# Graph mixture-of-experts kernel, edge stage: ScalarE's single rows fetched one round ahead, VectorE's and ScalarE's order inside a group changed

## The chip, the core and the metric

The kernel runs on one core of a Trainium2 chip. The metric is the device time of one execution in microseconds (us). Three executions of the kernel before took 2914.96, 2916.74 and 2917.04 us; the median is 2916.74 us.

## The reference, cut to what matters

`x` holds 6250 nodes of 256 features, `src` and `dst` 200000 edges sorted by `dst`. All arithmetic is float32.

```python
h = feats * rsqrt(deg_out)[:, None]
m = segment_sum(h[src], dst, num_segments=n) * rsqrt(deg_in)[:, None]
x1 = (m @ W_gc + b_gc) + (feats @ W_res + b_res)
# top-2 of 64 experts, each gelu(x @ w1 + b1) @ w2 + b2
y = x1 + moe(x1)
# normalise over nodes, add feats, LayerNorm over features
```

The change touches only the stage that computes `segment_sum(h[src], dst)`, the projection of each finished tile of 128 nodes and its routing to experts.

## The kernel before, in words

**Ahead of the edge stage** the kernel counts out-degrees, scales the nodes and writes them to `table` in HBM. SyncE (SP) issues those stores. For each group of edges it packs the first and last tile of nodes that the group's edges reach, and how many tiles are finished after it, into one integer, `code` (line 904).

**The edge stage** takes the edges in 196 groups of 1024 (`GROUPS`), each of 8 chunks of 128 (`CPG`). A round (`it`) is six groups, `q` = 0 to 5 (`RING`), and there are six ring buffers. Five engines work on it, each with its own loop:

- GpSimd (POOL) gathers one chunk of 128 rows of 1 KB per indirect DMA (line 516). It waits for the indices of the group (`idx_ready`) and for the sum of the group six before (`acc_added`, line 513), since that frees the buffer. In the sixth group (`q` = 5, `ROW_Q`) it gathers seven chunks; the rows of the eighth are fetched one by one by two other engines, so a round has 47 gathers.
- SP fetches 96 of these 128 rows with one DMA each into `row_buf` (lines 413 to 423) and then counts `rows_there`. It does so for round `it` once `rows_placed` says that round `it` - 2 was placed.
- ScalarE (ACT) per group: makes the indices for the same buffer of the next round (line 638), runs the group's tick if it has one, and in `q` = 0 to 3 loads 8 node numbers and issues 8 row DMAs straight into the ring buffer of `q` = 5 (lines 693 to 695). It can't start them before the last round's sixth group is summed (line 690). At the end of `q` = 3 it copies SP's 96 rows from `row_buf` into the ring buffer (line 702, `rows_placed`).
- VectorE (DVE) makes for each group the one-hot matrices that send an edge's row to its node: `dstq` (line 923) and `hot` (line 925), two buffers. If the group reaches a second tile it makes a second set, `dstx` and `hotx` (lines 934 and 936). It adds TensorE's results to `acc` (line 943 for the second tile, line 1048 for the first, which counts `acc_added`).
- TensorE (PE) multiplies the 8 one-hot matrices with the 8 gathered chunks (line 1258), called the main product below, and once more with `hotx` for a second tile. For `q` = 5 it also waits for `rows_placed` and `act_rows` (lines 1331 and 1332).

**A tick** follows a group that finishes a tile `i` (each group with a second tile here). All engines but POOL take part: ACT copies `x` and the tile's sums to `xS` and `mS` (lines 642 and 644) once `acc_added` has this group; DVE takes the in-degree (line 962) for ACT's square root (line 646). PE transposes four blocks (line 1275), and does the rank products of tile `i` - 2 (lines 1282 and 1283). ACT copies them to `tS` (line 650) and PE projects (line 1296). For tile `i` - 1 DVE forms `yS` (lines 971 and 973), PE transposes it (line 1289), ACT copies it to `ytS` (line 654), and PE computes the logits (line 1303). DVE does the placing of tile `i` - 2 (lines 980 to 1005), the choice of experts of tile `i` - 1 (from line 1012), and ends with a reciprocal (line 1029), after which ACT refines the root (lines 665 to 671).

**The order on VectorE** before, in `extras` and `pair`: load the group's code (line 309) and branch on it (line 944); if there is a second tile, make `hotx`, then (`later`) the one-hots of the next group, then wait for the second product and add it; without a second tile, only the one-hots of the next group. Then wait for the main product, add it (line 1048), and run the tick.

**After the edge stage** POOL waits for all 196 sums (line 526), clears its buffers (lines 527 to 529) and waits for the slot tables (line 532); then the experts run.

Of the kernel before, what the change touches and what calls it, by code (L numbers as in the profile page):

```python
# [9 lines left out]
ALU = mybir.AluOpType  # L10
# [4 lines left out]
P = 128  # L15
# [26 lines left out]
ACT_TURNS = (P - SP_ROWS) // ACT_ROWS  # L42
MAIN = 3
# [19 lines left out]
def graph_moe_kernel(nc, x, src, dst, W_gc, b_gc, W_res, b_res, Wg, bg, w1, b1, w2, b2, gamma, beta, out):  # L63
    ctx = ExitStack()
    with ctx:
# [531 lines left out]
        def _(act):  # L597
# [42 lines left out]
            def tick(i, behind, sums=GROUPS):  # L640
# [14 lines left out]
                behind(1, transposed_y)  # L655
                def keep_y(t):
# [16 lines left out]
            def group_ticks(g):  # L673
                ticks_of_group(act, group_code(act, g), lambda i, behind: tick(i, behind, g + 1))

# [7 lines left out]
            def fetch_rows(it, par, turn, first):  # L683
                r0 = SP_ROWS + turn * ACT_ROWS
                if turn == 0:
                    if first:
                        act.wait_ge(table_first, 16)
                        act.wait_ge(table_rest, 16 * (NB - 1))
                    else:
                        act.wait_ge(acc_added, it * RING)  # L690
                    act.wait_ge(listed, it * 16 + 16)
                    act.sem_inc(act_starts, 1)
                act.load(row_regs, row_list[0:1, bass.ds(par, 1), r0:r0 + ACT_ROWS])
                for r in range(ACT_ROWS):
                    act.dma_start(ring(ROW_Q)[r0 + r:r0 + r + 1, CPG - 1, 0:D], row_of(act, row_regs[r])).then_inc(act_rows, 16)  # L695
# [9 lines left out]
            def step(it, first):  # L705
                par = 0 if first else nc.s_assert_within(act.snap(it & 1), 0, 1,
                                                         skip_runtime_bounds_check_because="it is a parity")
# [770 lines left out]
```

## Time and profile before

| | |
|---|---|
| median of three runs | 2916.74 us |
| the profiled execution's own time | 2912.62 us |
| its span in the profile | 2910.8 us |
| busy share of the span | PE 71%, PEld (weight loads) 59%, DVE 42%, ACT 15%, POOL 64% |
| granted TensorE clock, mean | 0.833 of full |
| edge stage (first gather to last sum) | 210.05 to 2161.7 us |

The profile is one execution; times count from the start of its span. A row of the timeline gives the start, the duration, engine and line, the operation, and in brackets how long the engine had been idle and what ended that.
### The profile page before, as it was taken

Reading aid. Unit: us, or ns where it says so; the run is one execution under the profiler, and the core shown is the slowest. Engines: PE = TensorE matmul, PEld = TensorE weight load, DVE = VectorE, ACT = ScalarE, POOL = GpSimd, SP = SyncE. Lnnn points to the kernel's source line nnn. Section 1 sums busy time; section 2 is a strip of 40 time slices with the busy share of each in tenths; the row PEclk is TensorE's granted clock in tenths of the full one; section 3 lists DMA queues with packets and bytes.
Section 4 is the critical chain, followed back from the end, with each engine's and each line's share of the span. In section 5 each row is a group of like instructions: output and inputs, shape, how many; then the busy total and the mean of one; then the engine's idle time right before and its main releaser. Section 6 shows DMA issues by size and latency. Waiting matters only on the chain.

```text
span 2910.8 us, 57770 instructions
## 1 busy us (share of the span) xinstructions
PE 2063.8 (71%) x10204; PEld 1716.3 (59%) x10251; DVE 1223.3 (42%) x3115; ACT 444.0 (15%) x1390; POOL 1855.4 (64%) x1938
## 2 busy tenths in 40 slices
PE   8955556556666666767777768777766799999760
PEld 7954444445455555555556556565646788899650
DVE  8971112222323434344445455454553322222367
ACT  3010000000000101111111111111112223333213
POOL 0007777777777777777777777777715767777500
PEclk6557777888888878888988899998888999999885
DMA  8033333333333333333333333333314556666532
GB/s 301 0 99 109 109 108 107 108 110 109 109 109 110 112 109 110 111 111 111 113 111 113 112 113 113 112 115 112 112 31 139 168 166 204 198 197 202 188 113 88
DMA packets 211682, 361.84 MB, mean 124 GB/s; under 512 B 46696, under 2 KB 133558, under 8 KB 211534
## 3 DMA queue, kind: packets, MB, share of 16 engines
q0 software_dynamic: 92112, 226.49, 26.4%
q1 hardware_dynamic: 110266, 126.48, 13.5%
q10 hardware_dynamic: 9156, 7.48, 0.8%
q14 instruction: 127, 1.04, 0.1%
q8 instruction: 21, 0.34, 0.0%
HBM read 327.93 MB, written 57.52 MB: 132 GB/s over the span
## 4 chain that ended last, share of the span: by engine, by line
POOL 38%; PE 23%; issue 19%; DVE 9%; DMA 5%; DVEq 4%; ACTq 1%; POOLq 1%; ACT 1%; PEld 1%; SPq 0%; PEldq 0%
POOL ring L516 19%; POOL stage L516 18%; PE bank L1258 6%; PE bank L1379 6%; PE bank L1373 6%; PE bank L1238 3%; DMA y<-ring,slots 1%; DMA ring<-nodes,slots 1%; DMA stage<-y 1%; PE bank L1364 1%; DVE acc L1156 1%; DVE stage L839 1%; POOL y L551 1%; PEld bank L1448 1%; ACTq L695 1%
## 5 line engine op out<-in xcount | busy, mean ns | idle before, releaser
L516 POOL DMA_INDIRECT ring<-table,ring_idx x792 | 749.0, 946 | 242.1 <-issue 240.9
L516 POOL DMA_INDIRECT stage<-table,ring_idx x739 | 698.9, 946 | 225.1 <-issue 224.0
L1258 PE MATMUL bank<-stage 128*128 128x257 f32 x1030 | 323.1, 482 | 195.9 <-DMA stage<-table,ring_idx 87.1
L1258 PE MATMUL bank<-ring,hot 128*128 128x257 f32 x1056 | 316.1, 465 | 164.9 <-DMA ring<-table,ring_idx 119.2
L1258 PEld LDWEIGHTS bank<-stage 128*128 128x128 f32 x1030 | 249.9, 249 | 263.7 <-issue 132.4
L1258 PEld LDWEIGHTS bank<-ring,hot 128*128 128x128 f32 x1056 | 245.3, 238 | 229.5 <-issue 111.6
L1048 DVE TENSOR_TENSOR acc<-acc,bank 128x257 f32 x196 | 82.9, 423 | 491.1 <-PE bank L1258 464.2
L1373 PEld LDWEIGHTS bank<-ring,stage 128*128 128x128 f32 x1984 | 237.8, 197 | 9.7 <-issue 3.1
L1373 PE MATMUL bank<-ring,stage 128*128 128x128 f32 x1984 | 240.4, 281 | 2.4 <-DVE ring L1103 1.1
L1258 PE MATMUL bank<-ring,stage 128*128 128x257 f32 x528 | 170.6, 493 | 95.8 <-DMA ring<-table,ring_idx 70.7
L551 POOL DMA_INDIRECT y<-ring,slots x192 | 194.9, 1015 | 65.5 <-issue 48.6
L1379 PE MATMUL bank<-stage,ring 128*128 128x256 f32 x976 | 225.1, 384 | 8.8 <-ACT ring L737 7.3
L1258 PE MATMUL bank<-stage,hot 128*128 128x257 f32 x512 | 158.2, 476 | 91.5 <-DMA stage<-table,ring_idx 71.7
L1258 PEld LDWEIGHTS bank<-ring,stage 128*128 128x128 f32 x528 | 131.6, 256 | 132.3 <-issue 71.1
L1379 PEld LDWEIGHTS bank<-stage,ring 128*128 128x128 f32 x976 | 182.1, 192 | 34.1 <-issue 10.9
L1258 PEld LDWEIGHTS bank<-stage,hot 128*128 128x128 f32 x512 | 122.4, 245 | 124.9 <-issue 58.7
L737 ACT ACTIVATE ring<-bank,b1e 128x128 f32<-128x128 f32 x488 | 139.1, 368 | 356.3 <-PE bank L1373 356.3
L638 ACT ACTIVATE ring_idx<-srcT 128x8 int32 (+1 forms) x198 | 40.4, 206 | 930.2 <-DMA ring<-table,ring_idx 448.6
L541 POOL DMA_INDIRECT ring<-nodes,slots x129 | 137.3, 1064 | 67.7 <-issue 41.0
L1238 PE MATMUL bank<-stage 128*128 128x49 bf16 x1568 | 160.6, 279 | 6.6 <-DVE stage L839 5.7
L1238 PEld LDWEIGHTS bank<-stage 128*128 128x128 bf16 x1568 | 153.2, 150 | 14.1 <-DVE stage L839 13.6
L923 DVE TENSOR_SCALAR dstq<-dstT,neg_base 128x8 f32 (+1 forms) x196 | 48.7, 249 | 246.1 <-issue 240.8
(231 smaller groups left out, 2479.6 us busy)
## 6 DMA issues: line engine op xcount, KB each, us to landing
stage<-in_L_gnn_w_dram SPq DMA_DIRECT2D x128, 512.0 KB, 4.0
row_buf<-table SPq DMA_DIRECT2D x3072, 1.0 KB
stage<-table ACTq DMA_DIRECT2D x1024, 1.0 KB
ring<-table,ring_idx POOLq DMA_INDIRECT x792
y<-zeros SPq DMA_DIRECT2D x49, 256.0 KB, 2.4
stage<-y SPq DMA_DIRECT2D x14, 896.0 KB, 7.1
stage<-table,ring_idx POOLq DMA_INDIRECT x739
stage<-in_L_gnn_b_dram SPq DMA_DIRECT2D x64, 128.0 KB
```

The source lines that it names most:

```text
L516: pool.indirect_dma_start(out=ring(q)[:, j, 0:D], out_offset=None, in_=table[:, :], in_offset=bass.IndirectOffsetOnAxis(ap=ring_idx[:, q, ...
L541: pool.indirect_dma_start(out=xg[e % AHEAD][:, k, :], out_offset=None, in_=nodes[:, :], in_offset=bass.IndirectOffsetOnAxis(ap=gidx[:, col ...
L551: pool.indirect_dma_start(out=y2[:, :], out_offset=bass.IndirectOffsetOnAxis(ap=sidx[:, col:col + 1], axis=0), in_=outs[:, par, k, :], in_ ...
L638: act.activation(ring_idx[:, q, :], srcT[:, bass.ds((it * RING + q) * CPG, CPG)], ACT.Copy).then_inc(idx_ready, 1)
L695: act.dma_start(ring(ROW_Q)[r0 + r:r0 + r + 1, CPG - 1, 0:D], row_of(act, row_regs[r])).then_inc(act_rows, 16)
L737: last = act.activation(h1[:, k, j, :], banks[2 + k][:, j * P:(j + 1) * P], ACT.Gelu, bias=b1e[:, j:j + 1])
L923: dve.tensor_scalar(dstq[:, q, :], dstT[:, bass.ds(g * CPG, CPG)], neg_base[:, bass.ds(g, 1)], None, ALU.add)
L1048: dve.tensor_tensor(acc[:, bass.ds(first_tile, 1), :], acc[:, bass.ds(first_tile, 1), :], banks[q][:, 0:D + 1], ALU.add).then_inc(acc_adde ...
L1238: last = pe.matmul(banks[0][:, 0:HI], lo_hot[:, q, :, c], hi_hot[:, q, :, c], start=first and q == 0 and c == 0, stop=final and q == n - 1 ...
L1258: last = pe.matmul(bank[:, 0:D + 1], hots[:, j, :], ring(q)[:, j, :], start=j == 0, stop=j == n - 1)
L1373: last = pe.matmul(bank[:, j * P:(j + 1) * P], w1s[:, par, c, j * P:(j + 1) * P], xt[:, c, :], start=c == 0, stop=c == DK - 1)
L1379: last = pe.matmul(dst, h[:, j, :], w2s[:, par, j, :], start=j == 0, stop=j == HK - 1)
```

## The change

- ACT fetches its 32 single rows for round `it` + 1 in `q` = 1 to 4 of round `it`, into `row_buf` (now all 128 partitions), not into the ring. Those of round 0 are fetched ahead of all groups.
- ACT places all 128 rows with one copy at `q` = 1 (`PLACE_Q`) of the round, in round 0 at `q` = 4. That copy now waits for the sum of the last round's sixth group and for its own rows; PE no longer waits for `act_rows`.
- VectorE makes the one-hots of the next group first, before it loads the group's code. The second tile's rows come after that in a loop over the further tiles, with one more drain.
- In a tick ACT copies `mS` after DVE's in-degree (`nd_deg`), not after `acc_added`; and it copies `ytS` before `tS`, where it was the other way round.

```diff
@@ scalar: tick @@
                 if i is not None:
                     act.activation(xS[:, :], xs[:, bass.ds(i, 1), :], ACT.Copy)
-                    act.wait_ge(acc_added, sums)
+                    act.wait_ge(nd_deg, i + 1)
                     act.activation(mS[:, :], acc[:, bass.ds(i, 1), 0:D], ACT.Copy).then_inc(nd_in, 1)
-                    act.wait_ge(nd_deg, i + 1)
                     act.activation(tmp[:, bass.ds(i, 1)], deg[:, bass.ds(i, 1)], ACT.Sqrt).then_inc(nd_sqrt, 1)
-                if i is not None:
-                    act.wait_ge(nd_tr, i + 1)
-                    act.activation(tS[:, :, :], banks[3][:, :], ACT.Copy).then_inc(nd_t, 1)
                 def transposed_y(t):
                     act.wait_ge(nd_ytr, t + 1)
                     act.activation(ytS[:, :, :], banks[5][:, 0:D], ACT.Copy).then_inc(nd_yt, 1)
                 behind(1, transposed_y)
+                if i is not None:
+                    act.wait_ge(nd_tr, i + 1)
+                    act.activation(tS[:, :, :], banks[3][:, :], ACT.Copy).then_inc(nd_t, 1)
@@ scalar: rows @@
-            def fetch_rows(it, par, turn, first):
+            def fetch_rows(it, par, turn):
                 if turn == 0:
-                    if first:
-                        act.wait_ge(table_first, 16)
-                        act.wait_ge(table_rest, 16 * (NB - 1))
-                    else:
-                        act.wait_ge(acc_added, it * RING)
                     act.wait_ge(listed, it * 16 + 16)
...
-                    act.dma_start(ring(ROW_Q)[r0 + r:r0 + r + 1, CPG - 1, 0:D], row_of(act, row_regs[r])).then_inc(act_rows, 16)
+                    act.dma_start(row_buf[r0 + r:r0 + r + 1, bass.ds(par, 1), :], row_of(act, row_regs[r])).then_inc(act_rows, 16)
...
-            def place_rows(it, par):
+            def place_rows(it, par, first):
+                if not first:
+                    act.wait_ge(acc_added, it * RING)
+                    act.wait_ge(act_rows, it * (16 * (P - SP_ROWS)) + 16 * (P - SP_ROWS))
                 act.wait_ge(rows_there, it + 1)
-                act.activation(ring(ROW_Q)[0:SP_ROWS, CPG - 1, 0:D], row_buf[0:SP_ROWS, bass.ds(par, 1), :],
-                               ACT.Copy).then_inc(rows_placed, 1)
+                act.activation(ring(ROW_Q)[:, CPG - 1, 0:D], row_buf[:, bass.ds(par, 1), :], ACT.Copy).then_inc(rows_placed, 1)
...
-                    group_ticks(it * RING + q)
-                    if q < ACT_TURNS:
-                        fetch_rows(it, par, q, first)
-                    if q == ACT_TURNS - 1:
-                        place_rows(it, par)
+                    ticks_of_group(act, group_code(act, it * RING + q), tick)
+                    if q == (ROW_Q - 1 if first else PLACE_Q):
+                        place_rows(it, par, first)
+                    if rows and q > PLACE_Q - 1 and q - PLACE_Q < ACT_TURNS:
+                        fetch_rows(it + 1, other, q - PLACE_Q)
@@ vector @@
-            def extras(g, c, later):
+            def extras(g, c):
                 first_tile, last_tile = field(dve, c, 0), field(dve, c, 1)
-                    rows_of(second)
-                    later()
-                    sum_of(second)
...
+                with dve.If(last_tile > first_tile):
+                    with dve.Fori(first_tile + 1, last_tile + 1) as tile:
+                        t = a_tile(tile)
+                        dve.reg_add(extra, extra, 1)
+                        n = dve.snap(extra, min_val=1, max_val=GROUPS * NT)
+                        dve.drain()
+                        dve.tensor_scalar(dstx[:, :], dstT[:, bass.ds(g * CPG, CPG)], neg_tile[:, bass.ds(t, 1)], None, ALU.add)
+                        dve.drain()
+                        dve.tensor_tensor(hotx[:, :, :], ...).then_inc(hotx_ready, 1)
+                        dve.drain()
+                        dve.wait_ge(groupx_mm, n)
+                        dve.tensor_tensor(acc[:, bass.ds(t, 1), :], acc[:, bass.ds(t, 1), :], banks[2][:, 0:D + 1], ALU.add)
@@ vector: pair @@
-                    def later(q=q):
-                        if q + 1 < HOTS:
-                            one_hots(it, q + 1)
-                        elif not final:
-                            one_hots(it + 1, 0)
+                    if q + 1 < HOTS:
+                        one_hots(it, q + 1)
+                    elif not final:
+                        one_hots(it + 1, 0)
                     c = group_code(dve, g)
-                    first_tile = extras(g, c, later)
+                    first_tile = extras(g, c)
@@ tensor @@
                     if q == ROW_Q and not final:
                         pe.wait_ge(rows_placed, it + 1)
-                        pe.wait_ge(act_rows, it * (16 * (P - SP_ROWS)) + 16 * (P - SP_ROWS))
```

## Rows read from the trace of the kernel before

**Rows 1.** Waits of POOL: engine, line, waited for: us in total, times, longest.
```profile
POOL ring L516 <- issue: 240.9, 788, 1.0
...
POOL ring L527 <- DVE acc L1048: 38.0, 1, 38.0
```

**Rows 2.** Stretches, gathers of line 516: stretch, length, busy (count), PEclk, DMA share, GB/s.
```profile
208.00:1980.00 1772.00, 1338.64 (x1416) 0.84 0.38 110
208.00:2124.40 1916.40, 1447.92 (x1531) 0.84 0.38 110
```

**Rows 3.** The same stretches, sums of line 1048.
```profile
208.00:1980.00 1772.00, 75.69 (x179) 0.84 0.38 110
208.00:2124.40 1916.40, 80.76 (x191) 0.84 0.38 110
```

**Rows 4.** Timeline: sums of groups 179, 187, 189, 193; 193's tick ends.
```profile
1989.65 0.42 DVE L1048 TENSOR_TENSOR acc<-acc,bank 128x257 f32 x1 [0.26 <-issue]
...
2080.61 0.42 DVE L1048 TENSOR_TENSOR acc<-acc,bank 128x257 f32 x1 [0.26 <-issue]
...
2101.92 0.42 DVE L1048 TENSOR_TENSOR acc<-acc,bank 128x257 f32 x1 [0.26 <-issue]
...
2148.75 0.42 DVE L1048 TENSOR_TENSOR acc<-acc,bank 128x257 f32 x1 [0.26 <-issue]
...
2156.60 0.16 DVE L1029 RECIPROCAL rs<-tmp  x1
```

**Rows 5.** Timeline, groups 188 and 189: VectorE and TensorE.
```profile
2088.74 0.16 DVE L1029 RECIPROCAL rs<-tmp  x1
...
2090.60 0.23 DVE L923 TENSOR_SCALAR dstq<-dstT,neg_base 128x8 f32 x1 [1.70 <-issue]
...
2090.91 1.23 DVE L925 TENSOR_TENSOR stage<-bank,dstq 128x1024 f32<-128x1024 f32 x1
2092.19 5.42 PE L1258 MATMUL bank<-stage 128*128 128x257 f32 x16 [3.30 <-DVE stage L925]
2092.42 0.42 DVE L1048 TENSOR_TENSOR acc<-acc,bank 128x257 f32 x1 [0.29 <-issue]
...
2094.26 0.23 DVE L934 TENSOR_SCALAR dstx<-dstT,neg_tile 128x8 f32 x1 [1.41 <-issue]
...
2097.45 3.64 PE L1258 MATMUL bank<-stage,slots 128*128 128x257 f32 x16
```

**Rows 6.** Chain of waits: VectorE's sequencer (DVEq) between that reciprocal and the one-hots.
```profile
2089.25 0.32 DVEq L309
...
2090.33 0.04 DVEq L922
```

**Rows 7.** Stretches: PE, PEld, DVE, ACT, POOL busy (count), PEclk, DMA share, GB/s.
```profile
1950.60:1954.40 3.80, 3.75 (x16) 2.95 (x16) 1.66 (x3) 0.21 (x1) 2.84 (x3) 1.00 0.36 107
...
2092.20:2096.00 3.80, 3.80 (x10) 3.04 (x11) 2.02 (x4) 0.21 (x1) 2.89 (x4) 0.56 0.36 105
```

**Rows 8.** Waits of TensorE for the single rows (the row is named by its destination).
```profile
PE bank L1258 <- DMA stage<-table: 60.3, 11, 7.0
```

**Rows 9.** Timeline, group 191: TensorE.
```profile
2116.80 5.27 PE L1258 MATMUL bank<-stage 128*128 128x257 f32 x16 [6.51 <-DMA stage<-table]
```

**Rows 10.** Timeline, the tick around the sum at 2101.92: VectorE and ScalarE.
```profile
2100.84 0.42 ACT L642 ACTIVATE xS<-xs 128x256 f32 x1 [1.02 <-issue]
...
2102.58 0.15 DVE L962 TENSOR_SCALAR deg<-acc  x1 [0.24 <-issue]
...
2103.72 0.60 ACT L650 ACTIVATE tS<-bank 128x512 f32<-128x512 f32 x1 [0.65 <-PE bank L1275]
...
2104.55 0.38 ACT L654 ACTIVATE ytS<-bank 128x256 f32<-128x256 f32 x1 [0.24 <-PE bank L1289]
...
2107.84 0.22 DVE L1012 TENSOR_TENSOR lg<-bank,bgb 128x64 f32<-128x64 f32 x1
```

**Rows 11.** Timeline, SyncE: the single-row DMAs of one round.
```profile
1982.15 44.77 SPq L420 DMA_DIRECT2D row_buf<-table  x96
```

More of the change, by code:

```diff
@@ L638, in indices, with tick @@
                 act.activation(ring_idx[:, q, :], srcT[:, bass.ds((it * RING + q) * CPG, CPG)], ACT.Copy).then_inc(idx_ready, 1)
[L640 removed]
+            def tick(i, behind):
                 if i is not None:
                     act.activation(xS[:, :], xs[:, bass.ds(i, 1), :], ACT.Copy)
[L643 removed]
+                    act.wait_ge(nd_deg, i + 1)
                     act.activation(mS[:, :], acc[:, bass.ds(i, 1), 0:D], ACT.Copy).then_inc(nd_in, 1)
[L645 removed]
                     act.activation(tmp[:, bass.ds(i, 1)], deg[:, bass.ds(i, 1)], ACT.Sqrt).then_inc(nd_sqrt, 1)
[L648 to L650 removed]
                 def transposed_y(t):
@@ L710, in step @@
                     indices(it + ahead // RING, ahead % RING, first and ahead < RING)
-                    group_ticks(it * RING + q)
-                    if q < ACT_TURNS:
-                        fetch_rows(it, par, q, first)
-                    if q == ACT_TURNS - 1:
-                        place_rows(it, par)
+                    ticks_of_group(act, group_code(act, it * RING + q), tick)
[3 more added lines that the diff above has]
+                        fetch_rows(it + 1, other, q - PLACE_Q)
+            act.wait_ge(table_first, 16)
+            act.wait_ge(table_rest, 16 * (NB - 1))
+            for turn in range(ACT_TURNS):
+                fetch_rows(0, 0, turn)
+            act.wait_ge(act_rows, 16 * (P - SP_ROWS))
             step(0, True)
-            with act.Fori(1, STEPS - 1) as it:
+            with act.Fori(1, STEPS - 2) as it:
                 step(it, False)
+            step(STEPS - 2, False, False)
             it = STEPS - 1
             for q in range(LASTQ):
-                group_ticks(it * RING + q)
+                ticks_of_group(act, group_code(act, it * RING + q), tick)
             last_ticks(act, tick)
@@ L926, in one_hots @@
                                   dstq[:, q, :].unsqueeze(2).to_broadcast([P, CPG, P]), ALU.is_equal).then_inc(hot_ready, 1)
-            def extras(g, c, later):
+            def extras(g, c):
                 first_tile, last_tile = field(dve, c, 0), field(dve, c, 1)
-                def rows_of(t):
-                    dve.drain()
-                    dve.tensor_scalar(dstx[:, :], dstT[:, bass.ds(g * CPG, CPG)], neg_tile[:, bass.ds(t, 1)], None, ALU.add)
-                    dve.drain()
-                    dve.tensor_tensor(hotx[:, :, :], iota_ps.unsqueeze(1).to_broadcast([P, CPG, P]),
-                                      dstx[:, :].unsqueeze(2).to_broadcast([P, CPG, P]), ALU.is_equal).then_inc(hotx_ready, 1)
-                def sum_of(t):
-                    dve.reg_add(extra, extra, 1)
-                    n = dve.snap(extra, min_val=1, max_val=GROUPS * NT)
-                    dve.wait_ge(groupx_mm, n)
-                    dve.tensor_tensor(acc[:, bass.ds(t, 1), :], acc[:, bass.ds(t, 1), :], banks[2][:, 0:D + 1], ALU.add)
-                with dve.If(last_tile > first_tile):
-                    second = a_tile(first_tile + 1)
-                    rows_of(second)
-                    later()
-                    sum_of(second)
-                    with dve.If(last_tile > first_tile + 1):
-                        with dve.Fori(first_tile + 2, last_tile + 1) as tile:
-                            t = a_tile(tile)
-                            rows_of(t)
-                            sum_of(t)
-                with dve.Else():
-                    later()
@@ new lines, in extras @@
+                with dve.If(last_tile > first_tile):
+                    with dve.Fori(first_tile + 1, last_tile + 1) as tile:
[5 more added lines that the diff above has]
+                        dve.drain()
+                        dve.tensor_tensor(hotx[:, :, :], iota_ps.unsqueeze(1).to_broadcast([P, CPG, P]),
+                                          dstx[:, :].unsqueeze(2).to_broadcast([P, CPG, P]), ALU.is_equal).then_inc(hotx_ready, 1)
+                        dve.drain()
+                        dve.wait_ge(groupx_mm, n)
+                        dve.tensor_tensor(acc[:, bass.ds(t, 1), :], acc[:, bass.ds(t, 1), :],
+                                          banks[2][:, 0:D + 1], ALU.add)
```

10 lines of the change are left out of this document (5 added, 5 removed).

## The prediction

> **What bounds the kernel now.** I read the waits of POOL first. The 1531 gathers [rows 2] take 1448 us and stand 0.305 us apart for no reason but issue [rows 1]: one gather each 1.25 us. Nothing in the change touches them, so POOL sets the pace of the stage up to 2124.4 us, and most work saved on other engines there is worth nothing. But then POOL waits 38.0 us for the last sum [rows 1]. Counting gathers against sums shows why. At 1980 us 1416 gathers are issued and 179 groups summed, which used 29 x 47 + 5 x 8 = 1403 of them; at 2124.4 it is 1531 against 191 groups, 1497 gathers [rows 2, 3]. So the backlog grows from 13 to 34 gathers (43 us). The other engines are slower than POOL in the last stage, where a tile ends with nearly every second group, and what they owe is paid after the last gather. **The lag of a group** is the time from its last gather's end to its sum. Gathers after group 193 take (8 + 3) x 1.25 = 13.8 us, so its gathers ended at 2110.6; its sum stands at 2148.75 [rows 4]: lag 38.2. For group 179 (121 gathers before the end: 1973.1; sum 1989.65) it is 16.6. Only this lag can be won.
>
> **What one cycle is made of.** From 179 to 193 there are seven pairs of a plain group and one with a second tile and a tick. They take 159.1 us; their gathers 137.6 (19.7 a pair). Pair 188/189, from the sum at 2080.61 [rows 4]: VectorE's tick ends with the reciprocal 8.1 later, the one-hots start after 1.86 more and are ready at +11.5, TensorE starts the main product at +11.6, the second product 5.26 after that, and the sum follows 4.5 after its start [rows 5]: 21.3. TensorE was idle for 3.30 us ahead of the main product, and the granted clock over it is 0.56, mostly the 1.2 GHz level; the same product of an earlier pair (group 176) ran at 1.00, the 2.4 GHz level, in 3.75 us [rows 7], where its follower can start after some 3.5. So the order alone costs 21.3 - (5.26 - 3.5) = 19.5, hardly more than the gathers, and the fallen clock 1.8. A third cost comes once a round: ScalarE's last eight single rows arrive late where the tick falls on q = 3. Group 191 starts at 2116.80 [rows 9], while its one-hots were due 11.6 after 2101.92, at 2113.5: 3.3 us lost. TensorE's waits for these rows are 60.3 us in 11 rounds [rows 8], with idling in it that it would have had anyway; the late ones among the last groups are 179, 185 and 191. Per pair that adds up: 159.1 / 7 = 22.7 is 19.5 + 1.8 + 0.9 (two waits of 3.3 in seven pairs), and 0.5 where the clock fell for longer.
>
> **The change, part by part.**
> *Rows a round ahead.* ScalarE's eight loads and DMAs per turn stay 32 per round; the three late arrivals (3 x 3.3 = 9.9) go. New in their place: the copy at q = 1 waits for the sum of the last group of the round before, and behind it stand ScalarE's fetches, the indices and the next tick. Indices are a round ahead of POOL, so this costs nothing while the lag is under five groups; if that cover were gone, POOL would stop. Copying 128 rather than 96 partitions I take at 0, as the copies of both heights in this trace have 0.42 us a piece; bounds 0 to 0.1. SP's 96 DMAs take 44.8 us [rows 11] of a round of 47 x 1.25 = 58.8, and are released two groups earlier than now; I count it as nothing. In round 0 the fetch for round 1 at q = 1 waits for the list that SP loads after its first 96 rows, some 27 us; group 5 may start 2 to 3 us late, at a lag of 8 that closes again: 0.
> *One-hots first.* After a tick they no longer wait for code, fields and branch: 2090.33 - 2089.25 = 1.08 us [rows 6]. Main product at +10.5 rather than +11.6.
> *Second tile's rows later.* The plain group's sum comes at +10.7; the next one-hots 0.8 after it (1.84 [rows 5] less the moved 1.03) and take 0.3 + 1.23. In their shadow run code, branch and the loop's set-up; `dstx` starts 1.3 (nothing but the drain) to 2.3 (all register work behind it) after them, I take 1.6, as the register steps of [rows 6] fit beside 1.23 us of work. Then 0.3 + 1.23: `hotx` ready at +15.0. The main product ends at +14.0 at full clock, at +15.7 as in [rows 5]. So the second product starts at +15.0 or +15.7, the sum comes at 19.5 or 20.2.
> *Tick order.* `mS` waits for the in-degree at 2102.58 + 0.15: 0.4 later. TensorE's transposes and rank products move by as much, and VectorE, which uses these at once, by 0.3. `ytS` then ends near 2105.0 [rows 10], `tS`, now behind it, takes 0.60, and the projection starts at 2105.7, 1.3 later than now; the logits end at +6.1, where VectorE wants them at 2107.84 - 2101.92 = +5.92 [rows 10] plus that 0.3. So 0.3 a tick; bounds 0 and 1.3 (all of TensorE's delay). TensorE's next plain product, 1.3 later, ends at +9.7 and waits only about 1.1 us for the one-hots, not 3.3. That is where I expect the clock to stay up: the waits of 1.0 us inside ticks leave it at 1.00 now.
> *ScalarE between ticks at q = 1 and 3* has two fetches, as before. Its `xS` ends at 2101.26 [rows 10], 0.66 ahead of the sum. With a pair 0.8 to 1.5 shorter, a tick that ends 0.3 later and an `mS` due 0.4 later, it is late by 0 to 0.8; I take 0.3.
>
> **The sum.** With the tick's 0.3 a pair comes to 19.8 (clock up) or 20.5; with ScalarE's lateness in two pairs of three I take 20.7, the worse end, since I can't exclude falls elsewhere. Seven pairs: 144.9 - 137.6 = 7.3 us of growth instead of 21.5. At group 179 the lag is 16.6 less 3.3 for the rows, less 1.3 for the clock (1.8, damped since such a wait doesn't always cost it): 12.0 (the floor is about 10: 2.1 landing, 3.5 and 4.5 for the products). So 19.3 at group 193 instead of 38.2: 18.9 less. The last tick gives back 0.3, and one tick more runs beside gathers: 0.3 by their lengths (2088.74 - 2080.61 = 8.13 beside, 2156.60 - 2148.75 = 7.85 after the last, [rows 4, 5]). By the Trainium skill, "SBUF — State Buffer", section on who interferes with whom, VectorE and GpSimd share a port pair and the second to come "fully blocks"; with 0.95 us a gather, the tick's eight bf16 scalar operations could then lose up to 7.6 us in that one tick more, and the gain would be near 11. The two tick lengths don't bear that out. Total: -18.9 + 0.3 + 0.3 = -18.3. Against the profiled execution's own 2912.6 that gives 2894.3; the median of before is 4.1 above that execution, so against it 2898.4.
>
> **Rivals.**
> *Only the row waits go* (0.14). The clock falls as often as now, because the waits of TensorE only move into the tick and ahead of `hotx`, and the order gives nothing. For it: the second product waits 1.0 us more. Against: 1.08 us saved sit on the chain itself. Gain 9.9: 2906.8.
> *ScalarE becomes the bound* (0.07). It now has four fetches between q = 1 and 4, each 5.5 with the group's code; if tick and fetches leave it 2.0 late at each tick, it gives back 7 x 2.0 = 14 and the result is within noise: 2912 to 2918. For it: the estimate above is already 0.3 late. Against: between two ticks it has no more fetches than now, and it is 15% busy over the span.
> *Slower: the tick's new order* (0.06). Place: between `ytS` and the logits. If the clock falls in the longer gap ahead of the projection, projection and logits (2.4 us) double, VectorE waits for the logits 2.4 + 0.3 per tick and saves 1.08: 1.6 lost per pair, 7 pairs after 179 and some 5 before it that now don't recover, 12 x 1.6 = 19 less 9.9 for the rows: +9, 2926. It decides from the point where a tick grows by more than 1.08 + 9.9/12 = 1.9 us. Against it: waits of 1 us keep the clock up now.
> *The change doesn't do what it says* (0.03): TensorE waits for ScalarE at the round's last group as before, now for the copy; 2916.
>
> **Numbers.** Forecast 0.70 and its rivals 0.30. A measurement of this kernel can tell 0.2%, 5.8 us, from no change. Low end: 19.8 a pair, the clock always up, is a growth of 1.0 and a lag of 13.0, less 25.2 and 0.6 back: 2892. High end takes in the second rival's time and some of ScalarE's: 2911. Faster 0.85, same 0.09, slower 0.06.
>
> **What would show it.** Right: POOL's wait for line 1048 falls from 38 to about 19 us; no wait of TensorE for single rows; 188/189 takes 20 to 21 us, with a wait of about 1 us ahead of the main product and PEclk near 1.0 over it; reciprocal to `dstq` 0.8 instead of 1.86; `hotx` about 3 us after the hot's start; tick 8.4 long. The gathers keep 1.25 us. Wrong: ticks of 9 us or more, ScalarE's `mS` over 1.5 us after the sum, or a backlog at 2124 us still above 30 gathers.

## The result and the profile after

| | before | after |
|---|---|---|
| median of four runs | 2916.9 us | 2959.0 us |
| ratio, 95% interval | | 1.014 (1.0121 to 1.0159) |
| profiled execution's own time, span | 2912.6, 2910.8 | 2954.9, 2953.1 |
| gathers done | 2124.4 | 2153.7 |
| last sum | 2161.7 | 2200.8 |

The change makes the kernel 42 us slower, where 18 us less was forecast. I read the changed kernel's profile as the one before: first what POOL waits for.

Waits of the kernel after: engine, line, waited for: us in total, times, longest.

```profile
ACT ring_idx L639 <- issue: 836.0, 144, 32.2
PE bank L1263 <- ACT mS L645: 160.3, 49, 11.3
DVE junk L970 <- PE bank L1271: 98.6, 17, 10.5
DVE lg L1002 <- PE bank L1291: 55.5, 27, 6.3
POOL ring L528 <- DVE acc L1036: 47.8, 1, 47.8
POOL stage L517 <- ACT ring_idx L639: 19.7, 9, 7.8
POOL ring L517 <- ACT ring_idx L639: 9.8, 9, 6.1
```

The same view of the kernel before has these for them.

```profile
ACT ring_idx L638 <- issue: 283.0, 80, 5.3
PE bank L1275 <- ACT mS L644: 52.7, 49, 2.0
DVE lg L1012 <- PE bank L1303: 4.0, 3, 2.8
```

The wait for the last sum has grown by 47.8 - 38.0 [rows 1] = 9.8 us, and POOL now waits 19.7 + 9.8 = 29.5 us for ScalarE's gather indices, where it waited 0.3. Together 39.3; the last sum stands 39.1 later. The other rows name the engine behind both. TensorE waits three times as long for ScalarE's `mS`. VectorE stands 98.6 us for the rank products behind that transpose, where it stood 0.4. ScalarE has 553 us more of "issue" ahead of its indices. Much of that is a change of label, since the waits there for gathers to land fell from 647 to 273 us; by all causes ScalarE's idle time ahead of the indices grew from 930 to 1130 us, and its sequencer is what was busy in it, as the timeline below shows. The row of TensorE's waits for single rows [rows 8] has no counterpart; that part does what it should.

Stretches of the kernel after, gathers of line 517, then sums of line 1036: stretch, length, busy (count), PEclk, DMA share, GB/s.

```profile
208.00:1980.00 1772.00, 1331.97 (x1408) 0.82 0.39 110
208.00:2125.00 1917.00, 1427.47 (x1508) 0.83 0.38 109
...
208.00:1980.00 1772.00, 74.03 (x175) 0.82 0.39 110
208.00:2125.00 1917.00, 79.10 (x187) 0.83 0.38 109
```

Compare [rows 2, 3]: 187 sums used 31 x 47 + 8 = 1465 of 1508 gathers. The backlog is 43 where it was 34, though POOL has already lost 23 gathers to its waits. In the prediction's terms the lag of group 186 is 64.6 us (28.1 before), more than five groups of 10 us, and in the timeline POOL's longest waits for indices (6.1 and 7.8 us) lie just there, at 2064 and 2090 us.

What ScalarE does between two ticks is in its timeline (start, duration, then engine, line and operation), around the sum at 2100.16, whose tick it has to serve. The last row is TensorE's.

```profile
2090.82 5.85 ACTq L687 DMA_DIRECT2D row_buf<-table  x8
2096.82 0.21 ACT L639 ACTIVATE ring_idx<-srcT 128x8 int32 x1 [6.55 <-issue]
2098.86 5.83 ACTq L687 DMA_DIRECT2D row_buf<-table  x8
2104.99 0.21 ACT L639 ACTIVATE ring_idx<-srcT 128x8 int32 x1 [7.96 <-issue]
2106.05 0.42 ACT L643 ACTIVATE xS<-xs 128x256 f32 x1 [0.85 <-issue]
2106.38 0.40 ACT L645 ACTIVATE mS<-acc 128x256 f32 x1
...
2106.83 0.69 PE L1263 MATMUL bank<-ident,mS 128*128 128x128 f32 x2 [6.64 <-ACT mS L645]
```

The kernel before, ScalarE, two turns of the same kind:

```profile
1949.72 3.33 ACTq L695 DMA_DIRECT2D stage<-table  x8
1953.21 0.21 ACT L638 ACTIVATE ring_idx<-srcT 128x8 int32 x1 [4.26 <-issue]
1955.29 3.26 ACTq L695 DMA_DIRECT2D stage<-table  x8
```

Eight row DMAs keep the queue for 5.8 us instead of 3.3. A whole turn (indices, code, eight rows) is 8.2 us (2096.82 to 2104.99) instead of 5.5, and two turns lie between ticks. So `mS` starts 6.2 us after the sum that it serves; the tick, VectorE's one-hots and everything behind them wait. This tick is no exception: `mS` starts more than 1.5 us after its sum in 16 of the 49 ticks, 10.9 us at most; before it never did (1.0 us at most).

The view of one line gives the row DMAs their durations, shortest, median and longest in ns. First the kernel before, then after.

```profile
L695 ACTq DMA_DIRECT2D stage<-table x1024: 223/232/550, 224.0 to 2115.0; - x171
```

```profile
L687 ACTq DMA_DIRECT2D row_buf<-table x1024: 226/552/762, 209.9 to 2104.1; - x171
```

The profile's page has the packets, again before and then after: those of all queues, and the queue of ScalarE's DMAs (packets, MB, share).

```profile
DMA packets 211682, 361.84 MB, mean 124 GB/s; under 512 B 46696, under 2 KB 133558, under 8 KB 211534
q10 hardware_dynamic: 9156, 7.48, 0.8%
```

```profile
DMA packets 240485, 361.91 MB, mean 123 GB/s; under 512 B 76457, under 2 KB 162359, under 8 KB 240335
q10 hardware_dynamic: 37956, 7.54, 1.3%
```

The same 1024 rows take 28800 packets more: 960 x 30. By the trace's packet sizes, 960 of q10's 1 KB packets became 16 of 64 bytes each, and their one semaphore packet of 4 bytes became 16. It is the 960 rows of rounds 2 to 31. The 64 of rounds 0 and 1, whose destination `row_buf[r, par, :]` has a number for `par`, are still one packet and still 0.26 us in the mean; the 960 whose `par` is a register are not, and take 0.554 us. The trace also keeps the shape that each DMA instruction carries: 1 element of 1024 bytes for the 64, 16 elements of 64 bytes for the 960. So the row is already in 16 pieces in the program's instruction. The Trainium skill, page "DMA: Bandwidth & Descriptors", section "Why a DMA increments its semaphore by 16 and not by 1", says that software can split a contiguous pattern of one dimension so that it spreads over the DMA engines; this trace agrees, with 16 pieces. That the register brings it about, and what it costs, is for the runs below.

What the change does on VectorE and ahead of the main product is as forecast. The kernel after in the stretch of [rows 5], VectorE and TensorE, and then that stretch's clock in the view of stretches (columns as in [rows 7]).

```profile
2088.77 0.16 DVE L1019 RECIPROCAL rs<-tmp  x1
2089.47 0.23 DVE L924 TENSOR_SCALAR dstq<-dstT,neg_base 128x8 f32 x1 [0.54 <-issue]
...
2092.49 1.23 DVE L926 TENSOR_TENSOR hot<-bank,dstq 128x1024 f32<-128x1024 f32 x1
2093.99 0.23 DVE L938 TENSOR_SCALAR dstx<-dstT,neg_tile 128x8 f32 x1 [0.27 <-issue]
...
2091.06 3.75 PE L1246 MATMUL bank<-stage 128*128 128x257 f32 x16 [0.46 <-DVE stage L926]
...
2091.06:2094.81 3.75, 3.75 (x16) 2.95 (x16) 2.62 (x5) 0.00 (x0) 0.00 (x0) 1.00 0.07 21
```

Reciprocal to `dstq` 0.70 us (1.86 before), `dstx` 1.50 us after the start of `hot`, the main product at granted clock 1.00 after 0.46 us of idling instead of 0.56 after 3.30. All of it is won behind a tick that is several us late.

### The profile page after: what moved, and what is told of

The parts are those of the page before. It is cut to its first block, busy times and chain, and to the rows that moved or that the text cites. A ratio compares the mean times of both kernels' runs of the same rounds, so it can differ in the third digit from the quotient of the medians.

```text
span 2953.1 us, 57904 instructions
## 1 busy us (share of the span) xinstructions
PE 2081.2 (70%) x10204; PEld 1719.9 (58%) x10251; DVE 1236.9 (42%) x3115; ACT 430.7 (15%) x1390; POOL 1857.1 (63%) x1938
## 3 DMA queue, kind: packets, MB, share of 16 engines
q10 hardware_dynamic: 37956, 7.54, 1.3%
## 4 chain that ended last, share of the span: by engine, by line
POOL 28%; PE 26%; issue 17%; ACTq 10%; DVE 8%; DMA 4%; DVEq 3%; ACT 2%; PEld 1%; POOLq 0%; SPq 0%; PEldq 0%
POOL ring L517 14%; POOL stage L517 13%; ACTq L687 6%; PE bank L1366 6%; PE bank L1360 6%; PE bank L1246 4%; PE bank L1226 3%; PE bank L1284 3%; DMA y<-ring,slots 1%; PE bank L1263 1%; PE bank L1351 1%; DMA stage<-y 1%; ACTq L685 1%; ACTq L291 1%; POOL y L552 1%
## 5 line engine op out<-in xcount | busy, mean ns | idle before, releaser
L1246 PE MATMUL bank<-ring,hot 128*128 128x257 f32 x1056 | 306.4, 453 | 134.8 <-DMA ring<-table,ring_idx 124.6
L1246 PE MATMUL bank<-stage 128*128 128x257 f32 x1030 | 297.7, 452 | 133.0 <-DMA stage<-table,ring_idx 96.3
L1246 PEld LDWEIGHTS bank<-ring,hot 128*128 128x128 f32 x1056 | 238.7, 232 | 196.0 <-issue 108.6
L1246 PEld LDWEIGHTS bank<-stage 128*128 128x128 f32 x1030 | 232.2, 231 | 192.9 <-issue 93.8
L1036 DVE TENSOR_TENSOR acc<-acc,bank 128x257 f32 x196 | 82.9, 423 | 568.4 <-PE bank L1246 490.2
L1360 PEld LDWEIGHTS bank<-ring,stage 128*128 128x128 f32 x1984 | 236.1, 196 | 10.4 <-issue 4.3
L1246 PE MATMUL bank<-ring,stage 128*128 128x257 f32 x528 | 156.3, 461 | 72.9 <-DMA ring<-table,ring_idx 66.5
L1246 PEld LDWEIGHTS bank<-ring,stage 128*128 128x128 f32 x528 | 121.8, 236 | 104.3 <-issue 61.7
L944 DVE TENSOR_TENSOR acc<-acc,bank 128x257 f32 x48 | 20.3, 423 | 296.5 <-PE bank L1246 296.5
```

What stands on the lines that cost most here:

```text
L1036: dve.tensor_tensor(acc[:, bass.ds(first_tile, 1), :], acc[:, bass.ds(first_tile, 1), :], banks[q][:, 0:D + 1], ALU.add).then_inc(acc_adde ...
L1246: last = pe.matmul(bank[:, 0:D + 1], hots[:, j, :], ring(q)[:, j, :], start=j == 0, stop=j == n - 1)
L1360: last = pe.matmul(bank[:, j * P:(j + 1) * P], w1s[:, par, c, j * P:(j + 1) * P], xt[:, c, :], start=c == 0, stop=c == DK - 1)
```

## The experiments

**The theories.** T1: the register in the destination lengthens the issue, ScalarE is late at ticks, and the rest follows. T2: the new orders (one-hots first, the tick) cost it. T3: the place of the fetches and of the copy in the round costs it. The kernel before was measured beside each set of runs on the same chip, and the ratios are to that. Their 95% intervals are 3 to 5 us to either side.

### Constant addresses, and the parts by themselves

e1, the kernel after with two rounds written out, so that `par` is a number everywhere on ScalarE, in the row DMAs and also in the load of the node numbers and in the copy (the diff here leaves these two out):

```diff
-                    act.dma_start(row_buf[r0 + r:r0 + r + 1, bass.ds(par, 1), :], ...)
+                    act.dma_start(row_buf[r0 + r:r0 + r + 1, par, :], ...)
-            with act.Fori(1, STEPS - 2) as it:
-                step(it, False)
+            with act.Fori(0, (STEPS - 3) // 2) as i:
+                step(i * 2 + 1, False, True, 1)
+                step(i * 2 + 2, False, True, 0)
```

> The kernel after, but ScalarE's round loop is written out for two rounds at a time, so that the destination of each single-row DMA is a constant address instead of one that holds a register; everything else is as in after. T1 (the register in the destination splits each row DMA into 32 packets and makes its issue 0.55 instead of 0.26 us, and that makes ScalarE late at the ticks): the DMAs issue at 0.26 us each, a turn of eight takes about 3.3 us instead of 5.8, and the time falls from 2959 to about 2899 (2896 to 2902), below before. T2 (the new orders on VectorE and in the tick are what costs): the DMAs get shorter but the time stays above 2930. T3 (the place of the fetches and of the copy in the round costs): also above 2925.

e2, the kernel before with a register in the destination and nothing moved:

```diff
+                last = CPG - 1 if first else nc.s_assert_within(act.snap((it & 64) + (CPG - 1)), CPG - 1, CPG - 1, ...)
-                    act.dma_start(ring(ROW_Q)[r0 + r:r0 + r + 1, CPG - 1, 0:D], ...)
+                    act.dma_start(ring(ROW_Q)[r0 + r:r0 + r + 1, bass.ds(last, 1), 0:D], ...)
```

> The kernel before, but the ring address of ScalarE's single-row DMAs is computed through a register whose value is always the same; nothing moves. T1: the row DMAs issue at 0.55 us each and a round has 32 of them, ScalarE is late at ticks and with the single rows of the sixth group: slower than before by 20 to 70 us, about 2937 to 2987. T2 and T3: the issue gets longer, but the time stays within 6 us of before, 2911 to 2923.

e3, before with only the change's rows (`fetch_rows`, `place_rows`, `step`), at constant addresses as in e1:

```diff
-                    act.dma_start(ring(ROW_Q)[r0 + r:r0 + r + 1, CPG - 1, 0:D], ...)
+                    act.dma_start(row_buf[r0 + r:r0 + r + 1, par, :], ...)
...
+                act.activation(ring(ROW_Q)[:, CPG - 1, 0:D], row_buf[:, par, :], ACT.Copy).then_inc(rows_placed, 1)
...
-                        pe.wait_ge(act_rows, it * (16 * (P - SP_ROWS)) + 16 * (P - SP_ROWS))
```

> The kernel before with only the rows fetched a round ahead and placed at q = 1, at constant addresses; VectorE's and the tick's order as before. T1: TensorE's waits for the single rows go and nothing comes in their place: 10 to 14 us faster than before, about 2905. T2: also faster, as the orders are what costs. T3: slower than before, above 2925, since ScalarE waits for the sixth group's sum ahead of a tick.

e4, before with only the change's `extras` and `pair`:

```diff
-                    first_tile = extras(g, c, later)
+                    if q + 1 < HOTS:
+                        one_hots(it, q + 1)
...
+                    c = group_code(dve, g)
+                    first_tile = extras(g, c)
```

> The kernel before with only VectorE's new order (one-hots of the next group ahead of the code, second tile's rows after them). T1: 9 to 11 us faster than before, about 2907. T2: slower than before by 10 us or more. T3: says nothing on it, within 12 us of before.

| | median us | ratio to before (95%) |
|---|---|---|
| before | 2920.06 | |
| e1 all, constant | 2900.23 | 0.9938 (0.9921 to 0.9954) |
| e2 before, folded register | 2920.60 | 1.0003 (0.9994 to 1.0013) |
| e3 rows only, constant | 2905.27 | 0.9956 (0.9940 to 0.9973) |
| e4 one-hots only | 2908.83 | 0.9961 (0.9949 to 0.9974) |

e1 decides between the theories: with nothing changed but how `par` is written, 2959 becomes 2900, and the change wins. The row DMAs are again one packet each (q10: 9156). The orders and the place of the fetches (T2, T3) can't be what makes it slow. e3 and e4 say the same from the other side: each part alone is faster, by 12.8 and 11.4 us of 2917. e2 is a miss of mine. Its packets are those of before (q10: 9156) and so is the issue (3.26 us for eight). The value had one possible value, and the DMA came out as with a constant; I take it that the register was folded into one. So it tested nothing. e1 by itself can't say which of the three addresses with `par` matters; e14 below can, since there only the destination of the rows is changed.

### The register alone, and the tick alone

e5, e2 with a value that is always 7, as `par` is 0 or 1, but that was not folded (q10 has 38916 packets):

```diff
-                last = CPG - 1 if first else nc.s_assert_within(act.snap((it & 64) + (CPG - 1)), CPG - 1, CPG - 1, ...)
+                last = CPG - 1 if first else nc.s_assert_within(act.snap(par * par + (CPG - 1) - par), CPG - 2, CPG - 1, ...)
```

> The kernel before, but the destination of ScalarE's single rows is again computed through a register, now as 7 plus the parity squared less the parity, whose value is always 7 but which no compiler can know; nothing moves. In e2 the register had been folded into a constant (q10 kept its 9156 packets and the issue its 0.41 us spacing), so e2 tested nothing. T1: q10 has some 38000 packets, the row DMAs issue at 0.55 us each, a turn of eight takes 5.8 us instead of 3.3, and the kernel is slower than before by 20 to 70 us. T2, T3: issue longer, time within 6 us of before.

e6, e3 with the register:

```diff
-                    act.dma_start(row_buf[r0 + r:r0 + r + 1, par, :], ...)
+                    act.dma_start(row_buf[r0 + r:r0 + r + 1, bass.ds(par, 1), :], ...)
```

> As e3 (rows a round ahead, all other orders as before), but with the register in the destination, as the change has it. T1: 13 to 21 us slower than before and some 30 us slower than e3 (2905), about 2938. T2 (what costs are the new orders): as e3, faster than before. T1 without any effect of the orders would give the time of after, 2959.

e7, e1 with the tick's order of before, and e8, before with only the tick's order of the change (the same lines, the other way round):

```diff
-                    act.wait_ge(nd_deg, i + 1)
+                    act.wait_ge(acc_added, sums)
                     act.activation(mS[:, :], acc[:, bass.ds(i, 1), 0:D], ACT.Copy).then_inc(nd_in, 1)
...
+                if i is not None:
+                    act.wait_ge(nd_tr, i + 1)
+                    act.activation(tS[:, :, :], banks[3][:, :], ACT.Copy).then_inc(nd_t, 1)
                 def transposed_y(t):
...
-                if i is not None:
-                    act.wait_ge(nd_tr, i + 1)
-                    act.activation(tS[:, :, :], banks[3][:, :], ACT.Copy).then_inc(nd_t, 1)
```

> Rows a round ahead at constant addresses and the one-hots first, the tick's order as before. If the tick's new order costs what e1, e3 and e4 leave for it (14.8 and 11.2 won by the parts alone, 19.8 by all three together), this is 2 to 6 us faster than e1 (2900): 2894 to 2898. If the two gains overlap instead, because both shorten the same lag, it stays within 2 us of e1.

> The kernel before with only the tick's new order on ScalarE (mS behind the in-degree, ytS ahead of tS). My prediction: 0.3 us a tick, 2 us in all, within the noise of before (2916 to 2923). The rival that had the clock fall behind it: 12 to 20 us slower. T2: slower by more than 20.

When these four ran, the kernel before took 4238.6 us beside them, and when the same four kernels ran again as e9 to e12, 4305.4.

| kernel | ratio | ratio when run again |
|---|---|---|
| before, register | 1.0164 (e5) | 1.0174 (e9) |
| rows only, register | 1.0382 (e6) | 1.0396 (e10) |
| rows constant, one-hots | 1.0146 (e7) | 1.0128 (e11) |
| tick only | 1.0009 (e8) | 1.0001 (e12) |

These don't decide what I had asked, since another engine bounds the stage there. SyncE's 96 single rows, and ScalarE's wait for them, in e8:

```profile
1987.19 88.06 SPq L421 DMA_DIRECT2D row_buf<-table  x96
...
ACT stage L699 <- SPq L424: 774.4, 28, 44.0
```

A round's rows take 88 us instead of 44.8 [rows 11]; the trace has bursts there in which instructions of SyncE, even register moves, take or come 0.70 us apart. A round can't be shorter than its rows. Worth keeping is that e7, the best kernel where rows take 45 us, is 1.3 to 1.5% slower than before here. That it waits for SyncE's rows at `q` = 1 and not at `q` = 3, with the indices behind it, would explain it: POOL waits 1097 us for indices in e7 and 936 in e8. No run tried the copy at another `q`. What was expected of e9 to e12:

> The kernel of e5 again, since the kernel before took 4238.6 us on e5's chip, where SyncE's single rows were issued far apart and bounded the stage. T1: where before takes about 2917, row DMAs issue at 0.55 us, a turn of eight takes 5.8 us, and the kernel is slower than before by 20 to 70 us. T2, T3: within 6 us of before.

> The kernel of e6 again (rows a round ahead through a register, all orders as before), for the same reason. T1: 13 to 21 us slower than before, about 2935 to 2940, and some 30 us slower than e3. T2: as e3, faster than before.

> The kernel of e7 again (constant addresses, one-hots first, the tick's order as before), for the same reason. If the tick's new order costs what e1, e3 and e4 leave for it: 2 to 6 us faster than e1 (0.9938 of before), so a ratio of 0.992 to 0.993. If the gains overlap instead: the ratio of e1 within 0.001.

> The kernel of e8 again (only the tick's new order), for the same reason. My prediction: 2 us in all, within the noise of before. The rival that had the clock fall behind it: 12 to 20 us slower. T2: slower by more than 20.

### The same where the kernel before takes about 2917

e13 is the kernel of e7, e14 that of e5, e15 that of e6, e16 that of e8.

> The kernel of e7 and e11 (constant addresses, one-hots first, the tick's order as before), to be had where the kernel before takes about 2917. If the tick's new order costs what e1, e3 and e4 leave for it: a ratio of 0.992 to 0.993 (e1: 0.9938). If the gains overlap instead: 0.9938 within 0.001.

> The kernel of e5 and e9 (before, with a real register in the destination of ScalarE's rows). T1: where before takes about 2917, slower by 20 to 70 us. T2 and T3: within 6 us of before.

> The kernel of e6 and e10 (rows a round ahead through a register, every order as before), to be had where the kernel before takes about 2917. T1: 13 to 21 us slower than before and about 30 us slower than e3 (0.9956 of before): a ratio of 1.0045 to 1.0072. T2: as e3.

> The kernel of e8 and e12 (before with only the tick's new order). e1 against e13 leaves 5 us for the tick's order (18.2 against 12.4 us in POOL's wait for the last sum; VectorE waits 37.1 instead of 2.7 us for the logits): so 3 to 8 us slower than before. My prediction had 2.

e17, e1 with half of the tick's order:

```diff
-                    act.wait_ge(nd_deg, i + 1)
+                    act.wait_ge(acc_added, sums)
                     act.activation(mS[:, :], acc[:, bass.ds(i, 1), 0:D], ACT.Copy).then_inc(nd_in, 1)
+                    act.wait_ge(nd_deg, i + 1)
```

> e1 with only half of the tick's new order: ytS ahead of tS, but mS again behind the sum and not behind the in-degree. If the order of ytS and tS is what costs, since the projection and with it the logits wait for tS: as e1, a ratio of 0.993 to 0.995, POOL's wait for the last sum about 18 us. If the wait of mS is: as e13, 0.990 to 0.992, the wait about 12 us.

e18, the kernel after with one option more:

```diff
-                    act.dma_start(row_buf[r0 + r:r0 + r + 1, bass.ds(par, 1), :], row_of(act, row_regs[r])).then_inc(act_rows, 16)
+                    act.dma_start(row_buf[r0 + r:r0 + r + 1, bass.ds(par, 1), :], row_of(act, row_regs[r]), single_packet=True).then_inc(act_rows, 16)
```

> The kernel after, with the option on each single-row DMA that asks for one packet. If the option undoes the split: q10 back to some 9200 packets; and if it is the number of packets that makes the issue long, the issue falls to about 0.26 us and the time to about 2899. If the issue is long for the way the instruction is decoded: still 0.55 us a row and 2950 to 2965.

| | median us | before beside it | ratio (95%) | POOL's wait for the last sum |
|---|---|---|---|---|
| e13 rows constant, one-hots | 2894.86 | 2920.92 | 0.9911 (0.9897 to 0.9924) | 12.4 |
| e14 before, register | 2991.35 | 2920.92 | 1.0241 (1.0225 to 1.0256) | 56.8 |
| e15 rows only, register | 2940.57 | 2915.09 | 1.0086 (1.0069 to 1.0103) | 51.7 |
| e16 tick only | 2928.17 | 2915.09 | 1.0038 (1.0024 to 1.0051) | 52.3 |
| e17 e1, `ytS` first only | 2898.00 | 2915.09 | 0.9939 (0.9926 to 0.9952) | 16.9 |
| e18 after, one packet | 2953.63 (one run) | 2915.09 | | 49.0 |

**e14** is the cleanest statement of T1: nothing is moved, nothing added but a register in one address and the few register steps that make it, and the kernel before loses 70 us, the upper end of what I had expected. `mS` starts over 1.5 us after its sum in 15 of 49 ticks. From its page, and its waits:

```profile
q10 hardware_dynamic: 38916, 7.54, 1.3%
```

```profile
PE bank L1260 <- DMA stage<-table: 149.3, 17, 11.5
PE bank L1277 <- ACT mS L644: 129.1, 48, 10.0
POOL ring L527 <- DVE acc L1050: 56.8, 1, 56.8
POOL stage L516 <- ACT ring_idx L638: 19.7, 6, 6.9
POOL ring L516 <- ACT ring_idx L638: 19.1, 8, 6.6
```

These are the waits of after, with TensorE's wait for the single rows (149.3, against 60.3 [rows 8]) on top, since here the rows have a deadline in the same round. **e15** against e3: the register costs 0.0130 of 2917, or 38 us, when the rows are a round ahead; 70 when they aren't. So in these runs fetching ahead protects against a slow issue by about half. e15 lies just above what I had expected of it (1.0045 to 1.0072).

**e16 and e17** measure the tick. VectorE's wait for the logits grew from 4.0 us in 3 ticks to 36.2 in 20 (`DVE lg L1009 <- PE bank L1300`). Two ticks of e16, TensorE's projection and VectorE's logits in the timeline, the clock over the two projections in the view of stretches (PE, PEld, DVE, ACT, POOL busy, PEclk, DMA share, GB/s):

```profile
2075.68 1.78 PE L1293 MATMUL bank<-wgc,tS 128*128 128x256 f32 x4 [0.96 <-ACT tS L654]
2077.25 1.91 PE L1293 MATMUL bank<-wres,tS 128*128 128x256 f32 x4
...
2079.78 0.22 DVE L1009 TENSOR_TENSOR lg<-bank,bgb 128x64 f32<-128x64 f32 x1 [1.59 <-PE bank L1300]
...
2098.96 1.13 PE L1293 MATMUL bank<-wgc,tS 128*128 128x256 f32 x4 [0.96 <-ACT tS L654]
...
2075.67:2079.16 3.49, 3.48 (x10) 2.80 (x10) 2.21 (x10) 0.26 (x1) 2.67 (x3) 0.55 0.49 137
2098.95:2100.95 2.00, 1.99 (x10) 1.79 (x11) 1.69 (x9) 0.26 (x1) 1.39 (x3) 1.00 0.54 170
```

The kernel before, its projection in the tick of the sum at 2080.61:

```profile
2083.05:2084.96 1.91, 1.91 (x12) 1.71 (x11) 1.60 (x10) 0.80 (x2) 1.31 (x2) 1.00 0.44 139
```

In the last fifteen ticks of e16 the projection starts 3.6 to 3.8 us after the sum, 2.4 to 2.8 in before, and TensorE idles 0.96 us ahead of it, less than 0.1 in before. In five of the last fifteen ticks (one of fifteen before) the clock is near its lower level over it (0.55 to 0.61, mostly 1.2 GHz), and it takes 3.1 to 3.6 us instead of 2.0; those ticks last about 10.1 us, the others 8.3 to 8.8. The idle time and the fallen clock come together in this count; that the one brings about the other in those five ticks and not in the other ten is not shown. From group 100 on a tick has a mean of 9.09 us in e16 and 8.27 in before, from its sum to the end of the reciprocal. The order alone costs 11 us (0.0038 of 2917), more than the 3 to 8 expected. e17 has the ratio of e1 with `mS` back behind the sum, and VectorE still waits 28.8 us for the logits (37.1 in e1, 2.7 in e13): most of the cost is `ytS` ahead of `tS`, not the wait of `mS`.

**e13**, which leaves out that order and the register, has the shortest time of these runs: 26 us less than before, and by the ratios 67 less than after. Its ticks have a mean of 8.25 us, and over none of its last fifteen projections is the clock down. Its interval (0.9897 to 0.9924) just touches that of e1.

**e18**, a single run, leaves the packets as they are (q10 still 37956) and the issue too (median 552 ns). So whether the issue is long for the number of packets or for how a split instruction is decoded stays open.

## Why the prediction was wrong

**The step that failed** is the first of the change part by part: "ScalarE's eight loads and DMAs per turn stay 32 per round". Their number stayed, and I took their price to stay too, so the term stood at nothing without a reason. A row DMA into an address with a register has its own price, 0.554 us and 32 packets, and no row of the trace of before showed that form: every row DMA there, SyncE's and ScalarE's, had a constant destination (SyncE's are written out for the two values of `par`). I had bounded copies of another height and waits that the trace did not show, and this changed form, one line of the diff, had no bound. With it a turn is 8.2 us and not 5.5, and the sum of the step is +60 us (2959.0 against 0.9938 of 2916.9, which is 2898.8). All three signs that the prediction named for being wrong were there: ticks from group 100 on have a mean of 12.25 us, `mS` starts up to 10.9 us after the sum, and the backlog at 2125 us is 43 gathers.

**The rest of the sum came out, in part by luck.** The kernel in which only this term is taken out, e1, comes to 2898.8 on the scale of the runs before; the forecast was 2898.4. By its steps:

- *Lag.* Forecast 12.0 us at group 179 and 19.3 at 193; e1 has 10.2 and 19.0. From 179 to 193 its sums stand 1983.0 to 2129.3, 146.3 us, where 144.9 was forecast.
- *Rows a round ahead.* Forecast 9.9 us; e3 12.8 (interval 7.9 to 17.5).
- *One-hots first and second tile's rows later.* Not priced by themselves in lag; alone they bring 11.4 (e4). `dstx` was put 1.6 us after the start of `hot` and came after 1.50.
- *Tick order.* Forecast 0.3 us a tick, measured 0.8 a tick and 11 us in all where it is alone, about 8 (0.9938 less 0.9911, hardly more than the noise) beside the other parts. That is inside the bounds of 0 and 1.3, but I had only VectorE's slack right (the fast ticks grew by 0.24 on mean). I said that waits of 1.0 us leave the clock up, which the kernel before showed; with one more such wait it is down over the projection in five of the last fifteen ticks of e16, and in eight of e1's.
- *Luck.* The forecast gain of 18.3 us is 20.4 for rows, one-hots and second tile, less 7 x 0.3 = 2.1 for the tick's order. e13, which has all but that order, gains 26.0, and in e1 the order takes 8 of it back. Two misses of nearly 6 us cancel, and e1 meets the forecast to 0.4 us where its parts don't. Its ticks from group 100 on have a mean of 9.24 us, over the 9 that the prediction gave as a sign of being wrong.

**The cover that went.** The prediction named what would happen if the lag passed five groups: "POOL would stop". It did, for 29.5 us. It had been costed at nothing with that condition attached, and the condition was judged with the wrong turn length.

**The rivals.** *ScalarE becomes the bound* (0.07) was the true place, with the right signature: `mS` late after the sum. Its price was off, 14 us for 2.0 us at each of seven ticks: in the trace `mS` is over 1.5 us late in only 16 of 49 ticks, but by 6.2 us in the one shown, and from group 100 on a tick is 4.0 us longer on mean (12.25 against 8.27). Its argument against itself, no more fetches between two ticks than now, was true of their number only. *Slower: the tick's new order* (0.06) had the right place, the gap ahead of the projection, and e16 shows a cost there, 11 us alone where the rival had 19; it is not what made the change slow. *Only the row waits go* and *the change doesn't do what it says* are out: e13 wins 26 us, more than e3's 12.8 for the rows alone, and TensorE's waits for single rows are gone.

**What stays open.** With the register the new orders cost (after 1.014, e15 1.0086, so 16 us). Without it they don't: e1 against e3 is 5 us less, within the noise. That a late ScalarE takes away what the one-hots win and leaves what the tick costs would explain it. The second half is seen: VectorE waits for the logits 55.5 us in after and 13.3 in e15, 37.1 in e1 and 3.2 in e3. The first half no run separates. The register's cost was 70 us in e14 and 38 in e15. `mS` is waited for about as long in both (129.1 and 122.4 us); what differs most is TensorE's wait for the single rows (149.3 us in e14, none in e15) and POOL's for indices (38.8 and 8.9 us), and no run parts these two.

## What to carry to other kernels

When a diff turns a constant into a register inside a DMA's address, treat the DMA as a new instruction: look for one of that form in the trace, and where there is none, put a bound on its issue that is not zero. Here 32 DMAs per round at 0.3 us more each, on an engine that was 15% busy, cost 60 us, since they lie between two deadlines (in e14, where nothing else changed, 70 us). The busy share says nothing about such an engine; its time between two deadlines does. And if loops can be written out for the few values that the register takes, the form stays cheap: two rounds written out gave back all of it.

## What the runs showed of the hardware that was not expected

- A row of 1 KB into SBUF at an address with a register went as 16 packets of 64 bytes and 16 of 4 bytes, and held ScalarE's queue 0.554 us; at a constant address as one of each, 0.26 us. The address of the row in `table` has a register in both forms. With a register that an assertion leaves one value, the DMA went as with a constant (e2).
- The store `nodes<-yS`, whose destination in HBM has a register too, keeps the queue 0.37 to 0.40 us in both kernels and goes as 128 elements of 1 KB. So a register in a destination need not bring 0.55 us; its shape and its memory are others than the row's, and which of these matters is not shown.
- With TensorE idle 0.96 us ahead of the projection, the projection ran mostly at 1.2 GHz in five of the last fifteen ticks of e16; in the kernel before, with less than 0.1 us of idling there, it did in one.
- The same kernel took 2915 to 2921 us beside e1 to e4 and e13 to e18, and 4239 and 4305 us beside e5 to e12. It isn't the chip: the one that the record calls 4 gave 4239 us and, 25 minutes later, 2915. At 4239 and 4305 SyncE's instructions come 0.7 us apart in bursts, while a packet of a row takes the same 46 ns (median) as elsewhere. What causes this is not known.
